# Attention output kept transposed and scaled on GpSimd through DRAM, with 14 loads a head, in a one-core attention and expert kernel

## The chip, the cores and the metric

The kernel runs on one core of a Trainium2 chip. The metric is the device time of one execution in microseconds. Three runs of the kernel before took 882.96, 883.56 and 879.89 us, median 882.96. One more execution was taken with the hardware profiler; it took 887.1 us.

The engines are named as in the profile: PE (TensorE, matmuls), PEld (its weight loads), DVE (VectorE), ACT (ScalarE), POOL (GpSimd) and SP (SyncE, which here only issues transfers).

## The reference

The input x is 4 images of 32 x 32 tokens with 192 channels. Two residual blocks follow one another: attention, then a mixture of experts.

```python
qkv = layernorm(x) @ qkv_w.T + qkv_b           # 12 heads of 16 channels
bias = rel_h[:, :, :, :, None] + rel_w[:, :, :, None, :]   # from q and two tables, 32 rows + 32 columns
attn = softmax((q * scale) @ k.T + bias, axis=-1)          # 1024 x 1024 for each of 48 (head, image)
x = x + (attn @ v) @ proj_w.T + proj_b
t = layernorm(x)                               # 4096 tokens
gate = t @ Wg.T + bg                           # 8 experts, the best one is taken
h = silu(t @ W1[e].T) * (t @ W2[e].T)          # F = 469
x = x + probability * (h @ W3[e].T)
```

What the change touches is the attention's output `attn @ v`: its division by the sums of the softmax, and the way in which it gets to the projection `@ proj_w.T`, where the 192 channels must lie on partitions.

## The kernel before

The program has stages that follow one another with a barrier between them: project (to about 116 us of the trace), attention (to 646 us), gate (to 709 us), route (to about 740 us) and experts (to the end).

Project normalizes x, makes q, k and v, splits q and k into a high and a low half-precision part each and stores them to DRAM (`qk_split`), as well as the products of q with the position tables (`rel_split`). v stays on the core.

Attention works on 48 (head, image) pairs, called heads here; n counts them, the image is n % 4. A head has four buffers' worth of slots, and the loads of head n + 3 are issued in step n. SP issues them: 8 loads of k and q parts (L526, L527, L530) after a wait for the scores of the head before, the rows of maxima (L621), and 8 loads of position products (L541, L542). On TensorE a step has four parts u = 0 to 3. In each, four score matmuls (L796) of the head, two raw-score tiles for maxima (L762) of a head ahead, and the weighted values (L808) of four tiles of probabilities. VectorE takes the maximum of each raw tile (L913), eight a head, from two PSUM buffers. GpSimd copies the eight maxima four times (L658), TensorE transposes them (L787, in u = 1), ScalarE copies that out (L878), and SP stores it as a further row of the score operand. ScalarE takes the exponentials (L896) from three PSUM banks. The weighted values come out as 4 quarters of 32 rows x 256 queries: 16 channels, one row of sums and unused rows in each quarter. Sums come from a seventeenth column of ones in v.

The output's way is: ScalarE copies it out of PSUM (copy_out, L884), TensorE turns it by 16 small matmuls against the identity (turn_out, L819, in u = 2 of the next head), VectorE takes the reciprocal of the sums (L923) and multiplies (L928) into `att_sb`, tokens on partitions.

GpSimd also does work for the experts in the attention steps, in program order after the copies of the head: the W3 weights of 8 experts are split into high and low parts, one expert every five heads (L720, L721, store L722), and the tail and top rows of W1 and W2 (L681, L682, L687, L688, loads L697, L701). It copies the head's values with their column of sums into a zeroed buffer (L666).

Gate has 8 steps of 512 tokens. TensorE first turns `att_sb` (8 transposes a step, L1073), ScalarE copies the result (L1138), then TensorE projects (L1084), VectorE adds the residual (L1192) and takes the statistics; normalization, parts and gate products follow some steps behind.

A list of instructions for each engine is fixed when the kernel is built; the engines wait for one another by semaphores.

## Time and profile before

| | us |
|---|---|
| three runs | 879.89, 882.96, 883.56 |
| profiled execution | 887.1 |
| its span | 884.8 |
| PE, DVE, ACT, POOL busy | 785.4, 724.5, 608.8, 284.8 |
| attention, from the trace | about 116 to 646 |
| gate, from the trace | 646 to 709 |

The span is the time between the first and the last record of the core, and 2.3 us of the execution lie around it. Busy times are of one engine each and overlap. A stage's limit is read from the stage: the steady period of a head, or of a step, and the wait that ends last in it. TensorE's granted clock was full (1.00) between 300 and 400 us, which is its higher level of 2.4 GHz.

### The profile page before, as it was taken

Reading aid. Unit: us, or ns where it says so; the run is one execution under the profiler, and the core shown is the slowest. Engines: PE = TensorE matmul, PEld = TensorE weight load, DVE = VectorE, ACT = ScalarE, POOL = GpSimd, SP = SyncE. Lnnn points to the kernel's source line nnn. Section 1 sums busy time; section 2 is a strip of 40 time slices with the busy share of each in tenths; the row PEclk is TensorE's granted clock in tenths of the full one; section 3 lists DMA queues with packets and bytes.
Section 4 is the critical chain, followed back from the end, with each engine's and each line's share of the span. In section 5 each row is a group of like instructions: output and inputs, shape, how many; then the busy total and the mean of one; then the engine's idle time right before and its main releaser. Section 6 shows DMA issues by size and latency. Waiting matters only on the chain. (4 is left out here: it accounts for less than half of the span.)

```text
span 884.8 us, 32156 instructions
## 1 busy us (share of the span) xinstructions
PE 785.4 (89%) x11946; PEld 487.2 (55%) x11946; DVE 724.5 (82%) x1022; ACT 608.8 (69%) x1139; POOL 284.8 (32%) x437
## 2 busy tenths in 40 slices
PE   3999938999999999999999999999988617999994
PEld 1768802444444444444444444444478617999994
DVE  6876767998999999999999999899347485888883
ACT  3675605888888888888888888888845603544442
POOL 5530000023343423303232233421015304666662
PEclk9999956999999999999999999999989657999998
DMA  6255973345555545444454545543044402222310
GB/s 175 72 144 176 365 225 101 101 126 135 137 145 139 134 128 135 125 120 129 135 137 132 140 135 145 150 125 84 4 179 133 166 0 75 81 82 83 97 57 8
DMA packets 69738, 109.71 MB, mean 124 GB/s; under 512 B 20139, under 2 KB 36681, under 8 KB 68146
## 3 DMA queue, kind: packets, MB, share of 16 engines
q1 hardware_dynamic: 59120, 75.49, 30.5%
q0 software_dynamic: 9248, 26.51, 10.6%
q10 hardware_dynamic: 1314, 6.95, 2.1%
q8 instruction: 36, 0.59, 0.3%
q14 instruction: 20, 0.16, 0.1%
HBM read 77.58 MB, written 33.19 MB: 125 GB/s over the span
## 5 line engine op out<-in xcount | busy, mean ns | idle before, releaser
L913 DVE TENSOR_REDUCE neg_max<-max_ps 128x1 f16<-128x1024 f32 x384 | 451.9, 1221 | 41.6 <-PE max_ps L762 33.9
L896 ACT ACTIVATE probs<-ring_ps 128x512 f32<-128x512 f32 x768 | 413.7, 596 | 68.7 <-PE ring_ps L796 60.0
L796 PE MATMUL ring_ps<-q_side,k_side 113*32 113x512 f16 x3072 | 241.1, 386 | 11.6 <-DMA q_side<-rel_split 8.3
L808 PE MATMUL out_ps<-probs,values 128*32 128x256 f32 x3072 | 200.4, 380 | 0.2 <-ACT probs L896 0.2
L762 PE MATMUL max_ps<-k_side,q_side 48*128 48x256 f16 x1536 | 137.5, 280 | 18.0 <-ACT ident L871 9.3
L808 PEld LDWEIGHTS out_ps<-probs,values 128*32 128x32 f32 x3072 | 92.7, 110 | 70.9 <-issue 1.0
L796 PEld LDWEIGHTS ring_ps<-q_side,k_side 113*32 113x32 f16 x3072 | 73.2, 94 | 96.8 <-ACT probs L896 38.7
L658 POOL COPY max_copies<-neg_max 128x32 f16<-128x32 f16 x48 | 10.1, 210 | 350.4 <-DVE neg_max L913 350.4
L762 PEld LDWEIGHTS max_ps<-k_side,q_side 48*128 48x128 f16 x1536 | 49.1, 95 | 121.9 <-issue 70.1
L1467 PE MATMUL hid_ps<-slot_t,w_top 128*118 128x128 f16 x312 | 69.0, 221 | 0.8 <-ACT slot_t L1513 0.8
L1468 PE MATMUL hid_ps<-slot_t,w_top 128*118 128x128 f16 x312 | 68.8, 221 | 0.0
L1471 PE MATMUL hid_ps<-slot_t,w_tail 128*118 128x128 f16 x312 | 68.8, 221 | 0.0
L1469 PE MATMUL hid_ps<-slot_t,w_top 128*118 128x128 f16 x312 | 68.8, 220 | 0.0
L1470 PE MATMUL hid_ps<-slot_t,w_tail 128*118 128x128 f16 x312 | 68.8, 220 | 0.0
L1446 POOL DMA_INDIRECT out<-y,slot_token x39 | 42.0, 1076 | 47.7 <-issue 25.7
L1431 POOL DMA_INDIRECT slot_rows<-token_rows,slot_token x39 | 44.2, 1133 | 39.4 <-issue 39.4
L1530 ACT ACTIVATE hidden_hi<-hidden 118x512 f16<-118x512 f32 x39 | 24.6, 631 | 40.1 <-DVE hidden L1570 40.1
L1570 DVE TENSOR_TENSOR hidden<-hid_ps,silu 118x512 f32<-118x512 f32 x39 | 27.0, 692 | 22.2 <-PE hid_ps L1471 17.0
L1523 ACT ACTIVATE silu<-hid_ps 118x512 f32<-118x512 f32 x39 | 23.3, 597 | 28.0 <-PE hid_ps L1471 28.0
L1467 PEld LDWEIGHTS hid_ps<-slot_t,w_top 128*118 128x118 f16 x312 | 41.9, 134 | 1.0 <-issue 1.0
L1468 PEld LDWEIGHTS hid_ps<-slot_t,w_top 128*118 128x118 f16 x312 | 42.0, 135 | 0.0
L1469 PEld LDWEIGHTS hid_ps<-slot_t,w_top 128*118 128x118 f16 x312 | 41.9, 134 | 0.0
(230 smaller groups left out, 1357.0 us busy)
## 6 DMA issues: line engine op xcount, KB each, us to landing
q_side<-rel_split SPq DMA_DIRECT2D x384, 64.0 KB, 2.3
q_side<-qk_split SPq DMA_DIRECT2D x192, 64.0 KB, 2.5
rel_split<-expert_weights ACTq DMA_DIRECT2D x6, 1024.0 KB, 4.9
rel_split<-expert_weights SPq DMA_DIRECT2D x6, 1024.0 KB, 6.1
q_side<-qk_split SPq DMA_DIRECT2D x48, 128.0 KB, 2.8
k_side<-qk_split SPq DMA_DIRECT2D x144, 32.0 KB, 1.8
token_rows<-tn_parts SPq DMA_DIRECT2D x8, 512.0 KB, 3.4
expert_weights<-in_w_t POOLq DMA_DIRECT2D x32, 117.2 KB, 3.0
```

Source lines behind the costliest of these rows:

```text
L762: last = nc.tensor.matmul(max_ps[t % 2][:, keys], q_side[j][at:at + HIGH, quarter, t * P:(t + 1) * P], k_side[j][at:at + HIGH, keys], star ...
L796: last = nc.tensor.matmul(ring_ps[turn_of(k) % BANKS][at:at + COLS, :], k_side[slot(s)][:, tile * P + at:tile * P + at + COLS], queries, s ...
L808: last = nc.tensor.matmul(out_ps[quarter * 2 * HD:(quarter + 1) * 2 * HD, :], values[j][:, tile, :], probs[:, u % 2 * GROUP + 2 * i + quar ...
L896: nc.scalar.activation(probs[:, u % 2 * GROUP + i, :], ring_ps[turn_of(k) % BANKS][:], ACT.Exp).then_inc(exp_done, 1)
L913: nc.vector.tensor_reduce(neg_max[:, j % 2, t:t + 1], max_ps[t % 2][:], AX, ALU.max, negate=True).then_inc(tile_max, 1)
L1431: pool.indirect_dma_start(rows[:, j, :], None, g.token_rows, bass.IndirectOffsetOnAxis(ap=g.slot_token[:, n:n + 1], axis=0), bounds_check= ...
L1446: pool.indirect_dma_start(g.out_rows, bass.IndirectOffsetOnAxis(ap=g.slot_token[:, n:n + 1], axis=0), y[:, j, :], None, bounds_check=last_ ...
L1467: nc.tensor.matmul(out, w_top[:, j, h, 0, some], hi_top, start=True, stop=False, skip_group_check=True)
L1468: nc.tensor.matmul(out, w_top[:, j, h, 0, some], lo_top, start=False, stop=False, skip_group_check=True)
L1469: nc.tensor.matmul(out, w_top[:, j, h, 1, some], hi_top, start=False, stop=False, skip_group_check=True)
L1470: nc.tensor.matmul(out, w_tail[:, j, h, some], hi_tail, start=False, stop=False, skip_group_check=True)
L1471: last = nc.tensor.matmul(out, w_tail[:, j, h, some], lo_tail, start=False, stop=True, skip_group_check=True)
```

## The change

The turned output is no longer made. The weighted output stays transposed (channels on partitions), and the values buffers are filled with ones, so that the sums come out in 16 rows of each quarter. For each head:

- ScalarE copies the output to `out_t`, which now has two buffers.
- SP stores one row of sums of each quarter to DRAM and loads them as 128 x 8; VectorE takes the reciprocal; SP stores it and loads it again, spread over 32 rows of each quarter. These four transfers are distributed over the steps of this and the next heads.
- GpSimd multiplies `out_t` by the spread inverse (`scale_output`).
- SP places the result in a DRAM buffer `att_dram`, channels by tokens. In steps 28 to 31 and in step 47 eight transfers bring it back, as `att_t` with channels on partitions. The last head of each image is placed directly by four transfers within the core's memory, three of the four in the gate stage.

The loads of a head go from 16 to 14: low and high k parts come in one transfer, and two position loads in one. SP's loop of four heads is written out as 48. The gate stage projects from `att_t` and has no transposes and copies.

```diff
+    sp.dma_start(k[K_LO:K_LO + 2 * HD, :], g.qk_split[1, :, rows, :]).then_inc(inc, 16)
+    sp.dma_start(k[0:HD, :], g.qk_split[1, 1, rows, :]).then_inc(inc, 16)
...
+    if i:
+        both = g.rel_split[1, :, :, head, slot, :].rearrange("q (a r) n -> r q a n", a=2)
+        sp.dma_start(q[HD + HS:HD + 2 * HS, :, :], both).then_inc(inc, 16)
...
+def store_sums(sp, g, n):
+    sp.wait_ge(g.out_copied, n + 1)
+    sp.dma_start(g.sums_dram[n % 2], g.out_t[HD::2 * HD, n % 2, :]).then_inc(g.sums_stored[n % 2], 16)
...
+def spread_inverse(sp, g, n):
+    sp.wait_ge(g.inverse_stored[n % 2], 16 * (n // 2 + 1))
+    every_row = g.inverse_dram[n % 2].rearrange("q (o n) -> q o n", o=1).broadcast_to([4, 2 * HD, N // 4])
+    sp.dma_start(g.spread[:, n % 2, :], every_row).then_inc(g.inverse_spread[n % 2], 16)
...
+def scale_output(nc, pool, g, n):
+    pool.wait_ge(g.inverse_spread[n % 2], 16 * (n // 2 + 1))
...
+    nc.gpsimd.tensor_tensor(g.scaled[:, n % 2, :], g.out_t[:, n % 2, :], g.spread[:, n % 2, :], ALU.mult).then_inc(g.output_scaled, 1)
...
+def place_output(sp, g, n):
+    sp.wait_ge(g.output_scaled, n + 1)
...
+        by_quarter = g.att_dram[head, :, image * N:(image + 1) * N].rearrange("c (q n) -> q c n", q=4)
+        sp.dma_start(by_quarter, g.scaled[:, n % 2, :]).then_inc(g.placed[n % B], 16)
...
+                if s.before(3):
+                    place_output(sp, g, s.n - 3)
+                if s.before(2):
+                    store_inverse(sp, g, s.n - 2)
+                if s.before(1):
+                    store_sums(sp, g, s.n - 1)
+                if s.after(3):
+                    load_positions(sp, g, head(s, 3), slot(s, 3), 0)
                 if s.after(1):
                     store_max(s.n + 1, slot(s, 1))
+                if s.before(2):
+                    spread_inverse(sp, g, s.n - 2)
+                if s.before(1):
+                    load_sums(sp, g, s.n - 1)
                 if s.after(3):
-                    load_positions(sp, g, head(s, 3), slot(s, 3))
-
-            steps(sp, BH, SLOTS, step)
+                    load_positions(sp, g, head(s, 3), slot(s, 3), 1)
...
+            for n in range(BH):
+                step(Step(n, n // SLOTS, n % SLOTS, BH, True))
...
-                nc.gpsimd.tensor_copy(values[slot(s)][:, :, 0:VW], g.v_sb[:, head(s) + slot(s) * HEADS]).then_inc(values_ready, 1)
+                nc.gpsimd.tensor_copy(values[slot(s)][:, :, 0:HD], g.v_sb[:, head(s) + slot(s) * HEADS]).then_inc(values_ready, 1)
                 if s.after(1):
                     repeat_max(s.n + 1, slot(s, 1), s.before(1))
+                if s.before(2):
+                    scale_output(nc, pool, g, s.n - 2)
...
-                    if u == 2 and s.before(1):
-                        bank_free(s, TURNED_AT)
-                        turn_out(s.n - 1)
...
-                    if u == 2 and s.before(1):
-                        normalize(s.n - 1, head(s, -1), slot(s, -1), s.before(2))
+                    if u == 0 and s.before(2):
+                        invert_sums(nc, dve, g, slot(s, -2), head(s, -2), s.before(4))
...
             def project_out(s):
-                pe.wait_ge(at_ready, 2 * s + 2)
+                if s % 2 == 0:
+                    pe.wait_ge(g.outputs_loaded[s // 2], 32)
+                    pe.wait_ge(g.last_placed[s // 2], 64)
```

In the order of instructions, SP's list in one step of attention stood like this before (k_side and q_side are the score operands of a head, rel_split the position products; the rest of the step is six more position loads):

```order
L526 ISA [waits scores_ready]
L526 DMA k_side<-qk_split 16x1024
L526 ISA
L526 DMA k_side<-qk_split 16x1024 x2
L527 REGISTER_ALU
L527 DMA q_side<-qk_split 16x4x1024
L530 DMA q_side<-qk_split 16x2x1024
L530 ISA
L530 DMA q_side<-qk_split 16x2x1024 x3
L620 REGISTER_ALU
L621 DMA q_side<-max_rows 1x32x128 [waits max_copied]
```

The same step stands like this now:

```order
L522 DMA k_side<-qk_split 32x1x1024 [waits scores_ready]
L523 DMA k_side<-qk_split 16x1024
L524 DMA q_side<-qk_split 16x4x1024
L527 DMA q_side<-qk_split 16x2x1024 x4
L605 DMA att_dram<-scaled 4x32x256 [waits output_scaled]
L573 DMA inverse_dram<-inverse 128x8 [waits inverted]
L549 DMA sums_dram<-out_t 4x256 [waits out_copied]
L537 DMA q_side<-rel_split 16x2x1024 x2
L539 DMA q_side<-rel_split 16x2x1024
L697 DMA q_side<-max_rows 1x32x128 [waits max_copied]
L581 DMA spread<-inverse_dram 128x1x256 [waits inverse_stored1]
L556 DMA sums<-sums_dram 128x8 [waits sums_stored0]
```

Five transfers for the output stand among the loads now, each with a wait of its own, and the rows of maxima stand between the position loads instead of ahead of all of them.

On GpSimd, in a step with a W3 split and a tail split (the names are those of the weights; values is the buffer of the next head), this stood before:

```order
L658 COPY max_copies<-neg_max 128x32 [waits tile_max,max_t_ready]
L720 CAST w_parts<-w_whole 128x768 [waits w3_stored,w3_loaded]
L721 TENSOR_TENSOR w_parts<-w_whole,w_parts 128x768 [waits weights_split]
L722 DMA w_split<-w_parts 128x1536 [waits weights_split]
L681 CAST expert_weights<-expert_weights 128x469 [waits tail_loaded0]
L682 TENSOR_TENSOR expert_weights<-expert_weights 64x469 [waits weights_split]
L697 DMA expert_weights<-in_w_t 64x469 [waits weights_split]
L697 DMA expert_weights<-in_w_t 64x469
L666 COPY values<-v_sb 128x8x17 [waits group_done]
```

and this stands now:

```order
L754 COPY max_copies<-neg_max 128x32 [waits tile_max,max_t_ready]
L595 TENSOR_TENSOR scaled<-out_t,spread 128x256 [waits placed2,inverse_spread0]
L819 CAST att_t<-att_t 128x768 [waits w3_stored,w3_loaded]
L820 TENSOR_TENSOR att_t<-att_t 128x768 [waits weights_split]
L821 DMA w_split<-att_t 128x1536 [waits weights_split]
L779 CAST expert_weights<-expert_weights 128x469 [waits tail_loaded0]
L780 TENSOR_TENSOR expert_weights<-expert_weights 64x469 [waits weights_split]
L795 DMA expert_weights<-in_w_t 64x469 [waits weights_split]
L795 DMA expert_weights<-in_w_t 64x469
L762 COPY values<-v_sb 128x8x16 [waits group_done]
```

The product of the output stands between the copy of the maxima and the splits, and waits for the spread inverse.

## Rows read from the trace of the kernel before

**Rows 1.** Windows of attention: busy us and count by engine, clock, DMA share, GB/s.
```profile
300.00:400.00 100.00, 98.95 (x1704) 45.90 (x1706) 93.67 (x96) 87.91 (x175) 29.39 (x53) 1.00 0.47 128
```

**Rows 2.** Timeline of PE, the transposed maxima: start, us, engine, line, operation.
```profile
283.01 0.22 PE L787 MATMUL ring_ps<-ident,max_copies 128*32 128x128 f16 x1
293.35 0.22 PE L787 MATMUL ring_ps<-ident,max_copies 128*32 128x128 f16 x1
```

**Rows 3.** Timeline of DVE in one head, with idle time before and its releaser.
```profile
286.33 0.20 DVE L923 RECIPROCAL recip<-ring_ps 128x8 f32<-128x8 f32 x1
...
286.88 4.78 DVE L913 TENSOR_REDUCE neg_max<-max_ps 128x1 f16<-128x1024 f32 x4
291.89 4.86 DVE L913 TENSOR_REDUCE neg_max<-max_ps 128x1 f16<-128x1024 f32 x4 [0.23 <-PE max_ps L762]
```

**Rows 4.** Timeline of SP, DMA issues in several stretches.
```profile
25.50 0.59 SPq L225 DMA_DIRECT2D qk_split<-expert_weights  x1
...
133.62 0.42 SPq L541 DMA_DIRECT2D q_side<-rel_split  x1
134.08 0.42 SPq L542 DMA_DIRECT2D q_side<-rel_split  x1
...
268.16 1.85 SPq L526 DMA_DIRECT2D k_side<-qk_split  x3
...
382.27 1.30 SPq L526 DMA_DIRECT2D k_side<-qk_split  x3
```

**Rows 5.** Waits of the whole span: waiter, releaser, total us, count, longest.
```profile
SPq L621 <- ACT max_rows L878: 87.6, 48, 9.6
```

**Rows 6.** Timeline of POOL in a step with W3 and tail splits.
```profile
250.06 0.83 POOL L720 CAST w_parts<-w_whole 128x768 f16<-128x768 f32 x1
...
256.63 0.30 POOL L666 COPY values<-v_sb 128x136 f32<-128x136 f32 x1
```

**Rows 7.** Windows of the gate stage, columns as in rows 1.
```profile
654.00:662.00 8.00, 8.00 (x54) 7.92 (x53) 4.76 (x19) 2.36 (x5) 0.00 (x0) 0.96 0.54 183
...
680.00:690.00 10.00, 8.62 (x75) 8.27 (x74) 7.14 (x26) 4.46 (x9) 4.25 (x9) 0.83 0.45 152
```

**Rows 8.** Timelines of PE and ACT in the head from 391.65.
```profile
391.26 0.39 PE L796 MATMUL ring_ps<-q_side,k_side 113*32 113x512 f16 x4
...
396.50 1.04 PE L808 MATMUL out_ps<-probs,values 128*32 128x256 f32 x16
...
397.73 0.27 ACT L878 ACTIVATE max_rows<-ring_ps 32x128 f16<-32x128 f32 x1
```

**Rows 9.** DMA, window 23 to 29: queue's packets, MB, share; KB, us to landing.
```profile
q1 hardware_dynamic: 448, 0.39, 21.4%
...
qk_split<-expert_weights SPq DMA_DIRECT2D x2, 128.0 KB, 2.0
```

**Rows 10.** Groups of lines in attention on POOL: busy us, mean ns, idle before.
```profile
L688 POOL TENSOR_TENSOR expert_weights<-expert_weights 128x469 f16<-128x469 f32 x16 | 17.3, 1080 | 1.4
...
L721 POOL TENSOR_TENSOR w_parts<-w_whole,w_parts 128x768 f16<-128x768 f32 x8 | 13.2, 1644 | 0.7
```

**Rows 11.** The page's DMA issues: count, KB each, us from issue to landing.
```profile
q_side<-qk_split SPq DMA_DIRECT2D x48, 128.0 KB, 2.8
```

**Rows 12.** DMA, window 266 to 268: the queue of instruction packets.
```profile
q8 instruction: 1, 0.02, 3.8%
```

**Rows 13.** Groups of lines in the gate stage, the transposes.
```profile
L1073 PE MATMUL at_ps<-ident_sb,att_sb 128*96 128x128 f32 x64 | 10.1, 310 | 2.5 <-ACT at_bottom L1138 1.6 <-PEq L566 0.9
```

**Rows 14.** Timeline of the gate stage.
```profile
646.32 1.05 PE L1073 MATMUL at_ps<-ident_sb,att_sb 128*96 128x128 f32 x8 [0.91 <-PEq L566]
...
650.43 0.55 PEld L1084 LDWEIGHTS proj_ps<-proj_w_top,at_top 96*128 96x128 f32 x2
...
682.82 1.01 DVE L1192 TENSOR_TENSOR x_sb<-proj_ps,x_sb 128x384 f32<-128x384 f32 x2
```

**Rows 15.** DMA, window 300 to 400: SP's queue.
```profile
q1 hardware_dynamic: 7620, 9.73, 37.0%
```

224 lines of the change are left out of this document (121 added, 103 removed).

## The prediction

> **What bounds the kernel now.** I read the windows of the two stages that the change touches, first, then one head of attention engine by engine, then the queues. All sums are made on the profiled execution, 887.1 us (span 884.8 and 2.3 around it), which lies 4.1 us above the median of 882.96 that is to be predicted; a difference found on the first is carried to the second. The three runs differ by 3.7 us among themselves, so 0.5% (4.4 us) is about what can be told from no change.
>
> In attention TensorE shows 98.95 us busy of 100 [rows 1], but it is not what sets the pace: its work is pipelined, and it waits on buffers that VectorE empties. One head takes 293.35 - 283.01 = 10.34 us, from one transposition of the maxima to the next [rows 2]. VectorE does eight maxima in it, four in 4.78 us and four in 4.86 (1.195 us each as they overlap), then a reciprocal and a product out of PSUM; between the last maximum and the first of the next head lie 0.55 us, and only 0.23 us is a wait on TensorE [rows 3]. So VectorE holds the head: 4.78 + 0.23 + 4.86 + 0.5 = 10.3.
>
> Three engines run close behind. SP issues 17 transfers for each head: where they stand written out, one starts at 133.62 and the next at 134.08, so one in 0.46 us [rows 4], some 8 us of the 10.3, and most of the rest is the wait for the rows of maxima, 87.6 us in 48 heads, 1.8 each [rows 5]. GpSimd is idle for 70% of the stretch [rows 1], but in lumps: in a heavy head it goes from a W3 split that starts at 250.06 through a tail split to the values copy that ends at 256.93, with no gap but its own chain [rows 6]. The gate stage is another matter: between 654 and 662 TensorE is busy 8.00 us of 8.00 [rows 7].
>
> **The change, part by part.** Attention, engine by engine. I call S the moment when the scores of the previous head are all done (391.65 in the head shown, from 391.26 + 0.39 [rows 8]).
>
> VectorE loses the reciprocal and the product between PSUM and att_sb, 0.55 us a head, and gains a reciprocal of the same 128x8, from SBUF, which I price at the 0.20 us of the one removed [rows 3]. TensorE loses 16 small matmuls, which stood ahead of the maxima that VectorE waits 0.23 us for. VectorE's own floor is then 9.6 + 0.2 + a short wait, about 9.95 us, -0.39 a head. ScalarE's 16 exponentials and two copies stay: 87.91 us of 100 [rows 1], 9.1 a head, so it does not become the limit.
>
> SP goes from 17 issues a head to 20: 14 loads, the maxima, and five for the new way of the output (sums out, sums in, inverse out, inverse spread, output placed). Sixteen of them at 0.46 are 7.4 us, and four that touch 128 rows I price at the 0.59 us of a 128-row store of before [rows 4]: 2.4. Together 9.8 us, with next to no time left for its waits. So a head cannot be shorter than about 9.8 to 10.1 us, and can be longer if a wait is met: place and inverse wait on other engines that are early, but the spread waits for a store that was issued some 2.7 us before and takes 2.0 us to land (the price of a 128-row store [rows 9]). I take 10.1 us, -0.24 a head, where VectorE alone would give 9.95; the ends are 9.95 and 10.5 (four waits of 0.1 more). For the 36 heads with a steady period: -8.5 us.
>
> The new product on GpSimd, 128x256. The trace has products of 768 elements in 1.644 us and of 469 in 1.080 [rows 10], so 1.9 ns an element, and 256 take 0.68 us. The engine has room, but the place counts: it stands behind the copy of the maxima and ahead of the weight splits and of the next values copy. SP reaches the spread after seven product loads (3.3 us), place, inverse, sums, three position loads, and the maxima, which are ready at S + 6.35 (397.73 + 0.27 [rows 8]). The spread is issued at about S + 7.2, lands 2.8 us later (the price of a 128 KB load [rows 11]), the product ends at S + 10.7, and with SP's own lag of some 0.3 us at S + 11.0. Before, GpSimd began its splits at S + 4.4. TensorE takes the next head's values at its S + 4.85 (396.50 [rows 8]), so the splits and the values copy now have 10.1 + 4.85 - 11.0 = 4.0 us. The heavy heads need 6.8 (256.93 - 250.12 [rows 6]). There are five with W3 and a tail split together, of 6.3 to 6.8 us: 32.7 - 20 = 12.7 us of loss. Nine others of 4.2 to 5.5 us lose 0.6 each on average, 5.6 together. TensorE has nothing to do in that wait and VectorE sits behind its two buffers, so this loss is on the path: +18 us. Its bounds: with the spread landing in 2.0 us and no lag the splits have 4.9 us and the loss is 9; with 3.6 us to land it is about 30.
>
> SP's code. The loop of four heads becomes 48 written out, so its instructions are fetched anew. Before, an instruction packet in the window 266 to 268 goes with three k loads that take 1.85 us where they otherwise take 1.30 [rows 4, 12]. I count +1.5 us for the first eight heads, where GpSimd's and VectorE's own fetches already make SP late, and +2 for later fetches (four to six times 0.5), bounds 0 and 5. Eight loads of the placed output add 8 x 0.5 us of issue in five heads: +2, bounds 0 and 4. Two position loads fewer ahead of the first head: -1. The last three heads have no loads and gain VectorE's 0.35 each: -1.
>
> The gate. TensorE's 64 transposes go: 10.1 us busy and 2.5 waiting [rows 13], and ScalarE's 16 copies with them. At the stage's start the projection began at 650.43, after transposes from 646.32 on [rows 14]: with one step's own load and copy left out, 3.6 us earlier now, if the outputs are there. In the steps that follow, TensorE is full until 662 and still 86% busy from 680 to 690 [rows 7], so of the other six steps' transposes (7.6 us) I count 5.4. The sum is -9 us, bounds -5 and -12. The three last heads are scaled and placed beside the first gate steps: the last placement, issued in the third step, lands some 19 us into the stage by my count, and image 3 is projected from the seventh step on, whose first residual stood at 682.82 [rows 14], 36 us in and 27 with the gain. So it is hidden; were that cover gone it would cost up to 4. The end of attention loses the last turn and VectorE's 0.55 us behind it [rows 3]: -1. The project stage loses a GpSimd memset that nothing waited for: 0.
>
> Sum: -8.5 + 18 + 1.5 + 2 + 2 - 1 - 1 - 9 - 1 = +3 us. On the profiled execution that is 890.1, on the median 886.
>
> **Rivals.** (A) The new chain is absorbed, and the gain stays: the spread lands in 2.0 us, the splits lose 9, SP keeps up and a head takes 9.95. Sum: -13.9 + 9 + 1 - 9 - 1 - 2 = -16, 867 us. For it: 128 KB stores landed in 2.0 us [rows 9]; SP has 1.8 us of wait a head that it can give up [rows 5]. Against: 20 issues leave it nothing, and the splits' length is measured.
>
> (B) The transfers become the bound: the new ones lie unevenly on the 16 DMA engines. In 300 to 400 SP's queue filled 37.0% of the engines' time [rows 15], 3.8 us of each engine in a head if it lies evenly. The spread and the placed output move 128 KB in rows of 1 KB, and the merged k load 32 rows of 2 KB. If four engines had to carry the first two and two engines the third, the busiest would take 32 + 32 rows at 0.046 us each (6.0 us x 16 x 21.4% / 448 [rows 9]) and 14 more at 0.078 (100 x 16 x 37.0% / 7620 [rows 15]): 4 us more, 7.9 us of every 10.1 beside GpSimd's own transfers, and what is spread or loaded lands 0.8 us later or more. Then heads take 10.3, the splits have 3.2 us and lose 30: -1.3 + 30 + 1.5 + 2 + 2 - 1 - 1 - 9 - 1 = +22, less what a longer head gives back to GpSimd, say +20: 903 us. It decides from the point where a spread lands over 3.3 us after its issue. Against it: nothing in this trace shows an uneven queue, since the transfers of before all have slowest dimensions of 16, 32, 64 or 128 rows.
> The Trainium skill, page "DMA: Bandwidth & Descriptors", section "Why a DMA increments its semaphore by 16 and not by 1", says that a transfer uses the largest number of engines, up to 16, that divides the slowest dimension of both sides, and that transfers from SP take the lowest-numbered ones. By that rule the spread and the placement (four quarters on one side) would use 4 engines and the merged k load (two parts) 2, which is this rival; no run here shows it yet.
>
> (C) SP itself is the bound beyond what I count, at 0.5 us an issue and with a wait in each head: 10.5 a head, +6 instead of -8.5, while GpSimd has 0.4 us more in each heavy head and loses 14: +13.5, 896.
>
> **How the numbers follow.** Forecast, 886 us: 0.40, with a range of its own from 878 to 895 (the splits' loss 9 to 25). A, 867: 0.31. B, 903: 0.18. C, 896: 0.11. Within 0.5% is 878.5 to 887.4: over half of the forecast's case (0.21), a little of A and C (0.04): 0.25. Faster: A without its tail and a little of the forecast: 0.32. Slower: the rest, 0.43. The range that leaves out two in ten: from 865, which takes in most of A, to 906, beyond B's value.
>
> **What would show it.** Heads of 10.1 us where GpSimd has no split, and 12 to 13 us in the five heavy ones, with TensorE's matmuls of the weighted values waiting for the values copy there: the forecast. SP without idle time between heads. Heads of 9.95 and no wait for values: A. Packets of 1 KB rows on a few engines only, spread landing after 3.3 us or more, and waits of TensorE on loaded heads: B. The first residual 3 to 4 us after the gate's start instead of 7, and the stage some 9 us shorter: the gate's term. The forecast is wrong if the values copy is never late, or if all heads, heavy or not, are longer than before.

## The result, and the profile after

| | before | after |
|---|---|---|
| median, us | 883.09 (4 runs, 879.89 to 883.56) | 989.19 (4 runs, 987.1 to 989.91) |
| ratio, 95% interval | | 1.121 (1.1175 to 1.1246) |
| span of the profiled execution | 884.8 | 987.4 |
| first to last transposition of the maxima (47 heads) | 500.4 | 599.7 |
| from there to the end of the span | 255.9 | 261.6 |

The kernel became 12.1% slower. 886 us had been forecast, with 906 as the upper end of the range. The table's last rows come from the transposed maxima, once a head: before they ran from 128.47 to 628.90. After, the query for that tile gives operation, count, shortest, median and longest duration in ns, and first and last start in us:

```profile
L891 PE MATMUL ring_ps<-ident,max_copies x48: 218/219/314, 126.1 to 725.8; 128*32 128x128 f16 x48
```

So 99.3 us of the 102.6 were lost between heads: a mean head takes 12.76 us and took 10.65. The stretch from 300 to 400 that [rows 1] shows of before, and a bad head just behind it (busy us and count of PE, PEld, DVE, ACT, POOL, then clock, DMA share, GB/s):

```profile
300.00:400.00 100.00, 84.61 (x1288) 35.92 (x1288) 77.06 (x74) 74.46 (x146) 36.05 (x62) 0.95 0.52 136
401.00:412.00 11.00, 10.98 (x137) 4.57 (x141) 6.17 (x6) 6.41 (x13) 2.74 (x5) 0.73 0.32 91
```

No engine is busier, but for GpSimd with 6.7 us more, mostly of products. TensorE issued 1288 matmuls where it had issued 1704; some 155 of the difference are the 16 small ones a head that the change itself removes, the rest is lost pace. In the second row it is busy for 10.98 us of 11.00 at a granted clock of 0.73 in the mean, so part of the time at the lower of its two levels (1.2 instead of 2.4 GHz); between 300 and 400 the mean is 0.95, where it was 1.00 [rows 1]. Sixteen matmuls of the same kind, right behind a wait of 2.12 us and eight us later:

```profile
401.02 1.93 PE L912 MATMUL out_ps<-probs,values 128*32 128x256 f32 x16 [2.12 <-POOL values L762]
408.64 1.04 PE L912 MATMUL out_ps<-probs,values 128*32 128x256 f32 x16
```

So a stall is paid for again in the matmuls behind it. Over the whole run the scores and the weighted values kept TensorE busy for 471.7 us (L900 and L912) instead of 441.5 (L796 and L808 of before); what part of that lay on the path no run tells, but in e15 and e16 below, where the stalls are gone, the clock is 1.00 again.

The heads are not equally long. PE's timeline (start, us) shows three transpositions early on, and two with the loads of the placed output between them:

```profile
141.03 0.22 PE L891 MATMUL ring_ps<-ident,max_copies 128*32 128x128 f16 x1
151.19 0.22 PE L891 MATMUL ring_ps<-ident,max_copies 128*32 128x128 f16 x1
161.38 0.22 PE L891 MATMUL ring_ps<-ident,max_copies 128*32 128x128 f16 x1
...
513.74 0.22 PE L891 MATMUL ring_ps<-ident,max_copies 128*32 128x128 f16 x1
534.90 0.31 PE L891 MATMUL ring_ps<-ident,max_copies 128*32 128x128 f16 x1
```

The first two heads shown take 10.16 and 10.19 us, but they lie ahead of the first spread (issued at 164.2), so the new chain does not run in them yet. Of the 44 heads in which it runs, only the last (9.85) is under 10.3. Compared with the same heads of before, the seven with a W3 split lost 23 us together (they take 12.4 to 16.7), the 23 with a tail or top split 35 (median 11.8), the ten without any split 17 (median 11.4), and the four at the loads of the placed output 27 (68.6 instead of 41.8). So more than half of the loss lies in heads for which the forecast had none or little. The waits of the whole span (total us, count, longest) name what is late:

```profile
POOL scaled L595 <- DMA spread<-inverse_dram: 391.4, 48, 14.1
DVE neg_max L1003 <- PE max_ps L868: 151.0, 126, 6.0
...
SPq L581 <- DMA inverse_dram<-inverse: 53.0, 33, 6.9
SPq L697 <- ACT max_rows L967: 49.5, 28, 5.2
PE ring_ps L900 <- DMA q_side<-rel_split: 39.8, 31, 2.9
...
PE out_ps L912 <- POOL values L762: 31.3, 20, 3.9
```

GpSimd waits for the spread in every head. SP waits 53.0 us for the stored inverse, a wait that before did not have, and TensorE 39.8 for loaded positions, where it had waited 8.3, by the page of before:

```profile
L796 PE MATMUL ring_ps<-q_side,k_side 113*32 113x512 f16 x3072 | 241.1, 386 | 11.6 <-DMA q_side<-rel_split 8.3
```

How the waits close into a loop is read from one head with a W3 and a tail split, on SP (issues) and on GpSimd:

```profile
389.78 0.58 SPq L697 DMA_DIRECT2D q_side<-max_rows  x1
390.75 0.57 SPq L581 DMA_DIRECT2D spread<-inverse_dram  x1
403.45 0.58 SPq L697 DMA_DIRECT2D q_side<-max_rows  x1
404.07 0.57 SPq L581 DMA_DIRECT2D spread<-inverse_dram  x1
```

```profile
394.77 0.72 POOL L595 TENSOR_TENSOR scaled<-out_t,spread 128x256 f32<-128x256 f32 x1 [6.44 <-DMA spread<-inverse_dram]
395.44 0.82 POOL L819 CAST att_t<-att_t 128x768 f16<-128x768 f32 x1
...
400.68 0.29 POOL L762 COPY values<-v_sb 128x128 f32<-128x128 f32 x1
400.91 0.22 POOL L754 COPY max_copies<-neg_max 128x32 f16<-128x32 f16 x1
```

From one store of maxima to the next: 0.97 us to the issue of the spread, 4.02 until the product starts, 6.14 of product, splits and the values copy until the next head's maxima are copied, and 2.54 through TensorE's transposition and ScalarE's copy until SP stores them: 13.67 us. The next spread stands behind that store in SP's list. Every late microsecond thus comes back in the next head. Without the splits (395.44 to 400.68) the same loop would take 8.4 us, an estimate from these rows; it is shorter than a head then, so in the ten heads without splits other waits must hold, those of SP and of TensorE on loads.

The end of attention and the gate did not give what was forecast either (+5.7 instead of -10):

```profile
740.57 0.17 POOL L852 MEMSET expert_weights<- 128x48 f16 x1
...
748.16 0.98 PE L1164 MATMUL proj_ps<-proj_w_top,att_t 96*128 96x192 f32 x2 [7.36 <-PEq L645]
...
767.09 1.19 POOL L595 TENSOR_TENSOR scaled<-out_t,spread 128x256 f32<-128x256 f32 x1 [4.27 <-DMA spread<-inverse_dram]
```

GpSimd's last work of the stage ends at 740.74 and ScalarE's last copy at 741.24, and yet the projection starts only at 748.16, 7.4 us behind GpSimd; before, GpSimd had ended 17 us ahead of VectorE, and TensorE started 0.3 us behind VectorE (646.00, and 646.32 in [rows 14]). From the last transposition of the maxima to the start of the gate stage it is 22.4 us instead of 17.4, and from there to the sum that makes the gates 62.1 instead of 61.8, where 9 us less had been forecast. In the gate the products of the last heads wait for their spreads ahead of the normalization on the same engine.

### The profile page after: what moved, and what is told of

It reads as the page before. It is cut to its first block and busy times, and to the rows that moved or that the text cites. A ratio compares the mean times of both kernels' runs of the same rounds, so it can differ in the third digit from the quotient of the medians.

```text
span 987.4 us, 29463 instructions
## 1 busy us (share of the span) xinstructions
PE 806.7 (82%) x11114; PEld 472.0 (48%) x11114; DVE 713.6 (72%) x973; ACT 604.3 (61%) x1123; POOL 315.2 (32%) x485
## 5 line engine op out<-in xcount | busy, mean ns | idle before, releaser
L986 ACT ACTIVATE probs<-ring_ps 128x512 f32<-128x512 f32 x768 | 415.1, 595 | 104.3 <-PE ring_ps L900 99.3
L900 PE MATMUL ring_ps<-q_side,k_side 113*32 113x512 f16 x3072 | 255.5, 403 | 52.9 <-DMA q_side<-rel_split 39.8
L912 PE MATMUL out_ps<-probs,values 128*32 128x256 f32 x3072 | 216.2, 404 | 31.6 <-POOL values L762 31.3
L595 POOL TENSOR_TENSOR scaled<-out_t,spread 128x256 f32<-128x256 f32 x48 | 35.3, 736 | 391.4 <-DMA spread<-inverse_dram 391.4
L868 PE MATMUL max_ps<-k_side,q_side 48*128 48x256 f16 x1536 | 139.8, 291 | 17.6 <-DMA q_side<-rel_split 9.4
L912 PEld LDWEIGHTS out_ps<-probs,values 128*32 128x32 f32 x3072 | 95.2, 116 | 123.0 <-POOL values L762 44.5
L900 PEld LDWEIGHTS ring_ps<-q_side,k_side 113*32 113x32 f16 x3072 | 70.5, 97 | 163.0 <-issue 78.3
L868 PEld LDWEIGHTS max_ps<-k_side,q_side 48*128 48x128 f16 x1536 | 54.0, 98 | 118.8 <-issue 72.2
L967 ACT ACTIVATE max_rows<-ring_ps 32x128 f16<-32x128 f32 x48 | 12.8, 266 | 64.1 <-PE ring_ps L891 62.7
L1638 DVE TENSOR_TENSOR hidden<-hid_ps,silu 118x512 f32<-118x512 f32 x39 | 27.0, 692 | 22.3 <-PE hid_ps L1539 17.4
L1535 PEld LDWEIGHTS hid_ps<-slot_t,w_top 128*118 128x118 f16 x312 | 42.3, 136 | 1.0 <-issue 1.0
L1536 PEld LDWEIGHTS hid_ps<-slot_t,w_top 128*118 128x118 f16 x312 | 42.4, 136 | 0.0
L1539 PEld LDWEIGHTS hid_ps<-slot_t,w_tail 128*118 128x118 f16 x312 | 42.3, 136 | 0.0
```

What stands on the lines that cost most here:

```text
L868: last = nc.tensor.matmul(max_ps[t % 2][:, keys], q_side[j][at:at + HIGH, quarter, t * P:(t + 1) * P], k_side[j][at:at + HIGH, keys], star ...
L900: last = nc.tensor.matmul(ring_ps[turn_of(k) % BANKS][at:at + COLS, :], k_side[slot(s)][:, tile * P + at:tile * P + at + COLS], queries, s ...
L912: last = nc.tensor.matmul(out_ps[quarter * 2 * HD:(quarter + 1) * 2 * HD, :], values[j][:, tile, :], probs[:, u % 2 * GROUP + 2 * i + quar ...
L986: nc.scalar.activation(probs[:, u % 2 * GROUP + i, :], ring_ps[turn_of(k) % BANKS][:], ACT.Exp).then_inc(exp_done, 1)
L1535: nc.tensor.matmul(out, w_top[:, j, h, 0, some], hi_top, start=True, stop=False, skip_group_check=True)
L1536: nc.tensor.matmul(out, w_top[:, j, h, 0, some], lo_top, start=False, stop=False, skip_group_check=True)
```

## The experiments

The theories, numbered as in the expectations: (1) order: the product stands ahead of the splits and waits for a landing, a loop through GpSimd; (2) few engines: the spread, the placed output and the merged k load lie on few of the 16 DMA engines and delay what is queued with them (rival B); (3) SP: 19 to 20 issues and waits of its own in one ordered list. The ratio is always to the kernel before in runs on the same chip.

**e1: the product behind the splits.**

```diff
                 if s.after(1):
                     repeat_max(s.n + 1, slot(s, 1), s.before(1))
-                if s.before(2):
-                    scale_output(nc, pool, g, s.n - 2)
...
                     load_top(g, top, s.n)
+                if n >= 2:
+                    scale_output(nc, pool, g, n - 2)
```

> The product on GpSimd moves from ahead of the weight splits to behind them (and ahead of the next values copy), nothing else. Theory 1 (order): in the changed kernel the spread's landing and the product stand in a loop, SP's spread, product, splits, values and maxima copy, TensorE, ScalarE, SP's store of the maxima, spread again, so each head lasts as long as that loop (11.1 us with a tail split, 13.7 with W3 too). Behind the splits the landing is hidden: heads fall to the 10.2 to 10.5 us of SP's 20 issues, GpSimd's wait for the spread (391 us) falls below 200, and the time to 900 to 920 us; the four steps with loads of the placed output stay long. Theory 2 (few DMA engines): the transfers themselves are late, so the wait only moves; heads stay above 11.5 and the time above 945 us.

960.48 us, ratio 1.0876 (1.081 to 1.0941); a mean head takes 12.15. So the place is worth 29 of the 106 us, and 77 remain: not the 900 to 920 us of theory 1 alone. GpSimd's wait for the spread fell from 391 to 305 us only. SP's wait for the inverse stays:

```profile
SPq L581 <- DMA inverse_dram<-inverse: 52.4, 38, 4.5
...
PE ring_ps L900 <- DMA q_side<-rel_split: 62.7, 39, 4.2
```

**e2: the same transfers on more engines, e3: e1 and e2 together.** The k load is split again, the spread goes in four parts of 32 rows, the placed output lies in DRAM as 128 rows, and is loaded per head in 16 rows: 24 issues a head.

```diff
-    sp.dma_start(g.spread[:, n % 2, :], every_row).then_inc(g.inverse_spread[n % 2], 16)
+    for q in range(4):
+        sp.dma_start(g.spread[2 * HD * q:2 * HD * (q + 1), n % 2, :], every_row[q]).then_inc(g.inverse_spread[n % 2], 16)
...
-        sp.dma_start(by_quarter, g.scaled[:, n % 2, :]).then_inc(g.placed[n % B], 16)
+        sp.dma_start(g.att_dram[head, image], g.scaled[:, n % 2, :]).then_inc(g.placed[n % B], 16)
```

> The product stays ahead of the splits; every transfer that has a slowest dimension of 2, 4, 5 or 6 is reshaped so that it has 16 or more: the k load in two parts (15 loads), the spread in four parts, the placed output in rows of quarter and channel, and its loads head by head. SP has 24 issues a head. Theory 2 (few DMA engines): the spread lands in 2.8 us instead of 4.3 and the steps that load the placed output lose their stalls of 3 to 10 us each, and the attention stage ends 1.5 us after its last matmul instead of 7: 920 to 945 us. Theory 1 (order): the loop keeps its length but for the landing, and SP's 4 further issues (1.9 us) eat that: 955 to 985 us outside the four long steps' share, so at least 950.

> Both edits. If order and engines are separate losses, heads last as long as SP's 24 issues, 11.3 to 11.6 us, without heavy heads, and the time is 915 to 935 us. If order alone is the cause, it is slower than the kernel with the order alone by SP's 1.9 us a head, some 20 to 80 us; if engines alone, as fast as the one with the engines alone.

976.0, ratio 1.1051 (1.097 to 1.1133), and 967.71, 1.0957 (1.0891 to 1.1024). Both are slower than theory 2 and the sum of theories had it (920 to 945, and 915 to 935). The spread now lands 3.45 us after the first of its issues (4.1 in after, medians from issue to the product's start), but four more issues eat that: the median head of e3 takes 11.75, and 24 issues at 0.48 are 11.5. With e3 above e1, theory 2 looked refuted; by e14 to e16 below, the longer list had hidden it.

**e7: only the placed output in 128 rows and its loads by head, at 20 issues a head.**

```diff
-    sp.dma_start(g.att_t[0:HD * len(heads), c, tokens], g.att_dram[heads.start:heads.stop, 0:HD, tokens]).then_inc(g.outputs_loaded[image], 16)
+        sp.dma_start(dst, g.att_dram[head, image].rearrange("(q r) n -> r q n", q=4)[0:HD]).then_inc(g.outputs_loaded[image], 16)
```

> The changed kernel with only the placed output in rows of quarter and channel and loaded head by head in 16 rows. Theory 2: the four steps' stalls, 20 us together against their neighbours, fall to the 2.3 us of five more issues each, and the wait of 7 us at the end of attention goes; with placements on 16 engines the spread lands up to 1 us sooner: 950 to 965 us. Theory 1: the four steps stay long, since the loop through the spread is what is late there, and the time stays within 980 to 992.

959.62, ratio 1.0913 (1.0875 to 1.0951): 30 us back, as theory 2 had it. The spread still lands after 4.1 us. The four heads with output loads take 57.7 instead of 68.6, and SP's wait for the inverse falls from 53.0 to 25.6 us; 19 us of the gain lie in the other heads. That the old loads used few engines shows in after, in a window at the end of attention in which only such loads run (columns as above):

```profile
741.00:747.00 6.00, 0.00 (x0) 0.00 (x0) 0.00 (x0) 0.24 (x1) 0.00 (x0) 0.82 0.32 131
```

Four loads of 320 KB, with five heads as the slowest dimension on the DRAM side, are in flight together, and the share stays at 0.30 to 0.34 in each us from 741 to 750. Five of sixteen engines would be 0.31. By the Trainium skill, page "DMA: Bandwidth & Descriptors", section "Why a DMA increments its semaphore by 16 and not by 1", a transfer runs on the largest number of engines, up to 16, that divides the slowest dimension of both sides, which is five here; the trace agrees.

**e5: the chain stretched by one head** (four buffers of output, product and spread one head later, the spread at the end of SP's step), **e6: e5 with e7's edit, e8: e6 with the placement issued by GpSimd.**

```diff
+                if s.before(3):
+                    place_output(sp, g, s.n - 3)
...
+                if s.before(2):
+                    spread_inverse(sp, g, s.n - 2)
...
-                if s.before(2):
+                if s.before(3):
+                    scale_output(nc, pool, g, s.n - 3)
```

```diff
-                if s.before(3):
+                if s.n == BH - 1:
...
+                    if s.n - 3 < BH - B:
+                        place_output(pool, g, s.n - 3)
```

> The changed kernel with the output's chain stretched by one head, its transfers and sizes as they are: the spread is issued at the end of SP's step (behind all loads, so its wait stands in front of none of them), the product follows one head later at the place it had (out_t has four buffers, the product is written over the spread), and the placement stands behind the maxima. Theory 1 (order): neither the loop through GpSimd nor SP's wait for the inverse (53 us in the changed kernel, in 33 heads) is left, heads come down to SP's 20 issues, 10.2 to 10.5 us, except the four heads with loads of the placed output; time 895 to 915 us. Theory 2 (few DMA engines set the pace whatever the order): loads land late as before, heads stay above 11 us, time above 935 us.

> The stretched chain, and the placed output kept in rows of quarter and channel, so that its store has 128 rows on both sides and its loads come head by head in 16 rows (44 instead of 8); k load and spread stay on few engines. Theory 2 for the loads of the placed output: the four steps lose their stalls (20 us together) and the attention stage ends 1.5 us after its last instruction instead of 7: 865 to 890 us. If those steps were long for the order's sake, no further gain against the stretched chain alone.

> As the stretched chain with the placed output in rows, and in addition GpSimd issues the placement itself behind its product, so that SP has 19 issues a head. If SP's issues are what is left, heads come down by another 0.4 to 0.5 us, 18 to 22 us less than without this edit; if VectorE already holds the head at 10.0 us, no gain; if GpSimd's extra 0.9 us a head brings back late values in the heads with W3 and a tail split, these get longer by up to 1 us each.

945.58, ratio 1.0753 (1.0701 to 1.0806); 930.09, 1.0567 (1.0519 to 1.0615); 941.71, 1.0712 (1.0659 to 1.0766). Slack for the product gives 44 us, but no run comes near the forecasts of theory 1 (895 to 915) or of e6 (865 to 890), and e8, with an issue less on SP, is slower than e6 and not 20 us faster: SP's wait only changes its line. In e5 and in e8, where SP has an issue less (the second diff), it stands at the load of the sums:

```profile
SPq L556 <- DMA sums_dram<-out_t: 44.7, 35, 4.4
```

```profile
SPq L556 <- DMA sums_dram<-out_t: 60.7, 40, 4.7
```

**e9: e8 with all of SP's waits for landings at the end of its step, the output placed by quarters again and loaded in few large transfers, and in the gate stage the expert loads earlier and one more product; e10: after with the expert loads earlier in the gate stage.**

```diff
-                if s.before(1):
-                    load_sums(sp, g, s.n - 1)
...
+                if s.before(1):
+                    load_sums(sp, g, s.n - 1)
```

```diff
+            load_experts(sp, g, experts_loaded)
...
-                    load_experts(sp, g, experts_loaded)
```

> The stretched chain, with SP's list cut to 19 issues a head and every wait on a landing at its end: GpSimd issues the placement, the spread and then the load of the sums stand behind all loads. The placed output lies in rows of channels with one stride, so its 8 loads have 96 or 80 rows as slowest dimension. In the gate stage the loads of the expert weights come ahead of the last placements, and head 45's product moves from the end of attention to the gate's start. Theory 3 (SP's list is full and in order, 10.17 us of issue a head in the changed kernel, so that each of its waits lengthens the head): heads come down to VectorE's 9.9 to 10.1 us, except where GpSimd is late; attention is 20 to 25 us shorter than in the stretched kernel with rows, the barrier behind attention comes within 2 us, and the gate is 5 to 9 us shorter than before: 860 to 885 us. If few DMA engines (spread and k load are still on 4 and 2) make loads late whatever SP does, heads stay at 10.7 to 11.3 and the time above 905 us.

> The changed kernel with one move: the four loads of the expert weights go from behind the last placement in the gate stage to ahead of head 46's placement, as early as the chain allows. If these 3 MB are what makes the normalized rows late in the middle of the gate, the gate gets 4 to 7 us shorter and the time 982 to 985 us; if the last placements then come late, the gain is lost: 987 to 992 us.

938.95, ratio 1.0659 (1.0603 to 1.0715): no better than e8 within the intervals, and each run slower than each of e6. The wait has gone to the next engine with an ordered list, and SP waits 81.8 us for the inverse that comes of it:

```profile
DVE inverse L566 <- DMA sums<-sums_dram: 43.8, 35, 7.4
```

e10: 992.08, ratio 1.1248 (1.1181 to 1.1315), no gain. The way from the last transposition to the gates' sum is 83.3 us instead of 84.5, while GpSimd waits 9.10 us for the last spread instead of 4.27, so the last placement comes later. Whether the expert loads held the gate stays open.

**e4: before with the merged k load alone; e11: before with three tiny loads more in each head (20 issues).**

```diff
-    for at, src in ((0, k_hi), (K_LO, k_lo), (LOWER, k_hi)):
-        sp.dma_start(k[at:at + HD, :], src).then_inc(inc, 16)
+    sp.dma_start(k[0:HD, :], k_hi).then_inc(inc, 16)
+    sp.dma_start(k[K_LO:K_LO + 2 * HD, :], g.qk_split[1, :, bass.ds(slot * D + head * HD, HD), :]).then_inc(inc, 16)
```

```diff
+    for j in range(3):
+        sp.dma_start(g.spare[slot][:, 8 * j:8 * j + 8], g.rel_split[0, 0, 0:HS, head, slot, 0:8]).then_inc(inc, 16)
```

> The kernel before with one part of the change alone: low and high k parts of a head loaded by one transfer of 32 rows (15 loads a head instead of 16). Theory 2 in its strict form (two DMA engines carry it, and these two are late): heads get longer by 0.2 to 0.5 us, 890 to 905 us. Theory 1: one issue less on SP, which has 1.8 us of wait a head: 880 to 884 us, no change.

> The kernel before with three tiny loads more for each head (16 rows of 16 bytes into a spare buffer, issued behind the position loads; 20 issues a head on SP instead of 17, the count of the changed kernel), nothing else. If the count of issues alone costs what the changed kernel lost, heads go to 11 us and more and the time above 915 us. By theory 3 the count takes only the 1.8 us that SP waits in a head, since none of the new issues waits: heads of 10.3 to 10.6 us, 880 to 897 us.

e4: 883.23, ratio 1.0008 (0.9974 to 1.0043): the merged load costs nothing in the kernel before. e11: 898.46, ratio 1.0185 (1.0142 to 1.0229): three issues more that wait for nothing cost 17 us, and SP's slack for the maxima falls from 87.6 us [rows 5] to

```profile
SPq L623 <- ACT max_rows L880: 35.3, 32, 9.8
```

But TensorE counts these loads among those of the head and waits for the last of them:

```profile
PE ring_ps L798 <- DMA spare<-rel_split: 18.1, 19, 2.2
```

So three small loads a head, issue and landing together, cost a sixth of what the change cost; this run does not tell the two apart.

**e12 to e16: the waits and the uneven transfers taken away one after the other.** The number of issues and their bytes stay as in after (e14's and later ones' output loads are per head). The outputs are not divided by the right sums, and in e16 other rows of k are used too. Each cut of the diff is against the run before it. e12: the product is of `out_t` with itself, so it does not wait for this head's spread but for that of the head before. e13: the loads of sums and spread read inputs, so SP waits for no landing of this head's chain. e14: e7's edit. e15: the spread reads 128 rows. e16: the k load reads 32 rows that follow one another.

```diff
-    nc.gpsimd.tensor_tensor(g.scaled[:, n % 2, :], g.out_t[:, n % 2, :], g.spread[:, n % 2, :], ALU.mult)
+    nc.gpsimd.tensor_tensor(g.scaled[:, n % 2, :], g.out_t[:, n % 2, :], g.out_t[:, n % 2, :], ALU.mult)
...
-    sp.wait_ge(g.inverse_stored[n % 2], 16 * (n // 2 + 1))
-    every_row = g.inverse_dram[n % 2].rearrange("q (o n) -> q o n", o=1).broadcast_to([4, 2 * HD, N // 4])
+    every_row = g.w3_rows[0, 0:4, 0:N // 4].rearrange("q (o n) -> q o n", o=1).broadcast_to([4, 2 * HD, N // 4])
...
-    every_row = g.w3_rows[0, 0:4, 0:N // 4].rearrange("q (o n) -> q o n", o=1).broadcast_to([4, 2 * HD, N // 4])
+    every_row = g.w3_rows[0, :, 0:N // 4]
...
-    sp.dma_start(k[K_LO:K_LO + 2 * HD, :], g.qk_split[1, :, rows, :]).then_inc(inc, 16)
+    both = g.qk_split[1].rearrange("i r n -> (i r) n")[bass.ds(slot * D + head * HD, 2 * HD), :]
+    sp.dma_start(k[K_LO:K_LO + 2 * HD, :], both).then_inc(inc, 16)
```

> The changed kernel, with the product on GpSimd taken of the output with itself, so that it need not wait for the spread just issued (it waits for the one of the head before, which has landed); all transfers are still issued. What it leaves out: the division by the sums. Theory 1: the loop through GpSimd is gone and only SP's own wait for the inverse and its full list remain, 940 to 965 us, near the kernel whose product stands behind the splits (960). If GpSimd's wait costs nothing, above 980.

> As the kernel without the product's wait, and in addition the spread and the load of the sums read inputs of the same shape instead of what was just stored, so that SP waits for no landing of the chain either. The same 20 issues a head, the same bytes, the same few engines; left out: the division by the sums. If the waits for landings in the engines' ordered lists are the larger loss, it comes down to 905 to 930 us (20 issues cost 16 us in the kernel before, the four heads with loads of the placed output some 15, the gate 5). If the transfers themselves are the limit (uneven engines, late loads), it stays above 940 us.

> As the kernel with the chain cut, and the placed output in rows of quarter and channel, loaded head by head in 16 rows. If the transfers of the placed output on few engines are what is left besides the count of issues, 890 to 905 us; if not, no more than the 5 us that the end of attention gains.

> The kernel with the chain cut and the placed output in rows, and one thing more: the spread reads 128 different rows of an input instead of 4 rows 32 times, so that it moves the same 128 KB by the same one issue, but with a slowest dimension of 128 on both sides. Left out: the division by the sums. If the spread's place on 4 engines still makes the head's loads late (TensorE waited 47 us for position loads), 905 to 915 us and a shorter wait; if not, 920 to 926 as before.

> As the kernel with the even spread, and the merged k load reads 32 rows in a row instead of two times 16, so that it has a slowest dimension of 32 on both sides; same bytes, same issue. Left out besides the division: the right k rows (low parts stand where high parts should). Now no transfer of the head is on fewer than 16 engines but the 4 KB of sums. If uneven engines are what was left, 895 to 905 us, what 20 issues cost in the kernel before; if bytes and packets as such are, no change against the kernel with the even spread.

| | us | ratio (95%) | step |
|---|---|---|---|
| after | 989.19 | 1.121 (1.1175 to 1.1246) | |
| e12, no wait of GpSimd | 945.2 (a second run 961.35) | none | -44 |
| e13, no waits of SP for the chain | 930.81 | 1.0533 (1.0449 to 1.0617) | -14 |
| e14, placed output on 16 engines | 923.45 | 1.045 (1.0367 to 1.0532) | -7 |
| e15, spread on 16 engines | 886.67 | 1.006 (1.0029 to 1.009) | -37 |
| e16, merged k load on 16 engines | 881.55 | 1.0 (0.9977 to 1.0023) | -5 |

e12's two runs lie 16 us apart and the steps go by the shorter, so only the sum of the first two is firm, 58 us. The numbers of engines in the table are by the rule above. The 7 us of e14 are within the intervals of e13 and e14. The step to e15 is far outside them: of 923 us in e14, 37 (34 by the ratios) go with the shape of the spread, though each issue moves the same bytes and hardly anything of the chain is waited for but the loaded sums (VectorE, 12.5 us) and the inverse behind them (SP, 16.0). The spread, which from issue to use took 4.1 us in after, lands in e15 in

```profile
spread<-in_w_rows SPq DMA_DIRECT2D x48, 128.0 KB, 2.6
```

What the spread did to others shows in e14, in the loaded rows of a head, issued on SP and used on PE:

```profile
296.25 0.42 SPq L542 DMA_DIRECT2D q_side<-rel_split  x1
```

```profile
303.82 1.04 PE L908 MATMUL ring_ps<-q_side,k_side 113*32 113x512 f16 x8 [3.69 <-DMA q_side<-rel_split]
```

7.5 us lie between issue and use, with TensorE idle for the last 3.69; in the kernel before, the 64 KB position loads landed after 2.3 us in the median. TensorE's total wait for such loads in e14, e15 and e16, one row of each:

```profile
PE ring_ps L908 <- DMA q_side<-rel_split: 47.1, 29, 4.0
```

```profile
PE ring_ps L908 <- DMA q_side<-rel_split: 20.9, 22, 2.2
```

```profile
PE ring_ps L909 <- DMA q_side<-rel_split: 15.3, 17, 1.9
```

And it is not the bytes: from 150 to 550 after moved 131 GB/s at a share of 0.51, e16 more of both with no loss, at full clock:

```profile
150.00:550.00 400.00, 340.96 (x5070) 143.45 (x5066) 299.80 (x283) 290.38 (x567) 114.11 (x200) 0.93 0.51 131
```

```profile
150.00:550.00 400.00, 380.47 (x6030) 163.68 (x6030) 355.87 (x337) 344.33 (x675) 137.84 (x247) 1.00 0.62 158
```

Two things stay open. e15 also replaces four source rows that are each read 32 times by 128 rows, and no run tells that wholly apart from the engines; against it speaks e2, which reads the same four rows 32 times each, but in four transfers with 32 rows as slowest dimension, and whose product starts 2 us after the last of them is issued (the four issues take 1.97 us together). And in another order of removal the steps would have other sizes, since the same lateness is shared.

**e17: a complete version in which hardly anything waits for a fresh landing.** One transfer within the core's memory of 112 rows puts the sums beside the outputs (they stand 16 rows apart, in every quarter), VectorE inverts 112x256 in place, GpSimd multiplies a head later, the placed output goes by rows, and k in three loads: 19 issues.

```diff
+    sp.dma_start(g.spread[0:P - HD, n % 2, :], g.out_t[HD:P, n % 2, :]).then_inc(g.inverse_spread[n % 2], 16)
...
+    sums = g.spread[0:P - HD, slot % 2, :]
+    nc.vector.reciprocal(sums, sums).then_inc(g.inverted, 1)
```

> A kernel that computes the reference and keeps the transposed output, drawn from the findings: no transfer of a head on fewer than 16 engines and no wait on a fresh landing in an ordered list. One transfer within the core's memory moves rows 16 to 127 of the output to rows 0 to 111 (112 rows on both sides), which puts each quarter's sums beside its outputs and replaces four transfers through DRAM; VectorE takes the reciprocal of 112x256 two parts later, GpSimd multiplies one head later, the placement has 112 rows and the outputs are loaded head by head in 16 rows, one a step. 15 loads a head, 19 issues. If uneven engines and waits were the whole loss, heads take 10.2 to 10.4 us (VectorE's reciprocal is longer by some 0.15 us than the one of 8 columns), the gate is 5 to 9 us shorter than before, and the time is 865 to 880 us. If the added 400 KB a head as such cost, heads are above 10.6 and the time above 890 us.

914.02 us, ratio 1.0342 (1.03 to 1.0385). All heads, those with W3 splits too, are now alike, but long: 11.35, from PE's timeline, and the reason stands in the groups by line (busy us, mean ns, idle time before and its releaser):

```profile
303.55 0.22 PE L876 MATMUL ring_ps<-ident,max_copies 128*32 128x128 f16 x1
314.90 0.22 PE L876 MATMUL ring_ps<-ident,max_copies 128*32 128x128 f16 x1
```

```profile
L560 DVE RECIPROCAL spread<-spread 112x256 f32<-112x256 f32 x48 | 83.7, 1743 | 9.6 <-DMA spread<-out_t 9.6
```

1.74 us on the engine that holds the head, where 0.15 more than the old reciprocal had been expected: with the maxima of [rows 3], 4.78 + 4.86 + 1.74 are 11.38. The chain's landings are no longer the matter: VectorE waits for them 9.6 us in 48 heads, and between 150 and 550 not at all. The gate, by contrast, did what was forecast: from the last transposition of the maxima to the sum that makes the gates it took 79.2 us before, 84.5 in after, and 69.8 here.

**e18: e17 with the inversion as a power of -1 on GpSimd.**

```diff
-    nc.vector.reciprocal(sums, sums).then_inc(g.inverted, 1)
+    nc.gpsimd.tensor_tensor(sums, sums, g.minus[0:P - HD, 0:1].broadcast_to([P - HD, N // 4]), ALU.pow).then_inc(g.inverted, 1)
```

> The kernel with the shifted sums, whose heads all took 11.35 us because VectorE's reciprocal of 112x256 takes 1.74 us; here GpSimd takes the reciprocal instead, as a power with the exponent -1, in front of the copy of the maxima, where it is idle for some 4 us of a head. If that power takes under 3 us, heads fall to 10.2 us, the gate keeps its 9 us, and the time is 858 to 872 us, below both kernels. If it takes 5 us or more, it is late for the copy of the maxima in each head and heads go above 11 us again: over 900 us.

2557.55 us, ratio 2.8983 (2.8914 to 2.9051): a miss, as one such operation takes 41 us.

```profile
L560 POOL TENSOR_TENSOR spread<-spread,minus 112x256 f32<-112x256 f32 x48 | 1975.2, 41150 | 2.6 <-DMA spread<-out_t 2.5
```

No complete version was faster than the kernel before.

## Why the prediction was wrong

- **The undisturbed head**, 10.1 us, was right where nothing waits: in e16, with all 20 issues, 23 of 47 heads take 10.25 us or less, most of them 10.18 or 10.19. In after, only the last head with the chain running was under 10.3, so the sign that the prediction named against itself, all heads longer whether heavy or not, came true but for the last. VectorE's floor of 9.95 was not reached in e16 either.
- **The landings** were the first step that failed. The spread was priced at 2.8 us from a 128 KB load in even rows [rows 11]; from issue to the product's start it took 4.1 in the median. The store of the inverse was priced at 2.0 us [rows 9], issued 2.7 ahead, so that SP would not wait for it; it landed after 4.4 in after and after 1.7 in e16:

```profile
inverse_dram<-inverse SPq DMA_DIRECT2D x48, 4.0 KB, 4.4
```

```profile
inverse_dram<-inverse SPq DMA_DIRECT2D x48, 4.0 KB, 1.7
```

- **Rival B** was named with its mechanism and its sign, a spread that lands after 3.3 us, and the sign came. It got 0.18 because no transfer of before was uneven; that absence was no evidence against it, since the change made such transfers for the first time. Its size was wrong by half: +20, against the 42 us that e15 and e16 took off. It was worked out from the mean load of the busiest engine (7.9 us of 10.1). What counts is how late a load becomes that is queued with it, and for whom: 7.5 us in e14.
- **The splits' loss, "+18"**, took lateness as something that a window of 4.0 us absorbs and that ends with the head. In the heavy heads it is a loop: the spread is issued behind the maxima, which wait for the GpSimd list, which waits for the spread. e1 and e12, which open the loop in different places, are 29 and about 44 us faster.
- **SP's added waits** were held to be nothing ("place and inverse wait on other engines that are early", and the inverse's store landed by the time of the spread). The engines are early, but the store has to land: 53.0 us of waits in an ordered list with all loads behind it, on an engine whose issues fill the head (nineteen in 9.6 us, from 379.65 on). e12 and e13 together took 58 us off.
- **The count of issues** was in the head's 10.1, and e16 bears that out; e11 shows that SP's slack was worth something all the same, 17 us for three small loads more in before. The forecast let SP give its slack away without a loss.
- **The loads of the placed output**, +2: their four heads grew by 26.7 us, part of it what all heads lost. On few engines, as the window from 741 to 747 shows; e7 took 10.9 of it off, and even in e16 the four take 50.3 instead of 41.8.
- **The gate and the end of attention**, -9 and -1: the size was right (e17: 69.8 us instead of 79.2, -9.4), but in after nothing of it came (+5.7 from the last head to the end). The end of attention lost 5.0 us, as GpSimd ended late and the next stage began 7.1 us behind it; the gate stage kept its 62 us, as the last products and their landings stood ahead of the normalization: without their waits it takes 56.0 us in e13 and 54.3 in e14. The prediction had named this cover and priced its loss at up to 4.
- **SP's written-out code**, +3.5, was not measured by itself, and no row shows the share of the other engines' fetches in it. e16 has it, and its attention takes 505.5 us (125.8 to 631.3) instead of 500.4: 5 us for it, the added issues, the output's loads and the splits together, less what shorter heads gave back.

## What to carry to other kernels

Before a transfer is added, work out over how many DMA engines it spreads, from the slowest dimension on both sides, and put its price on the loads that share its queue. A wait for a landing in an engine's ordered list holds all that is behind it, and moving it to another engine moves the loss (SP in after, e5 and e8, VectorE in e9); follow it round until it either ends or comes back to its own start. A price read from transfers of one shape holds for that shape and for a queue as empty as it was. A gain at a stage's border counts only if no other engine becomes the one that the border waits for.

## What the runs showed of the hardware that was not expected

- A reciprocal on VectorE takes 1.743 us for 112x256, and 0.20 for 128x8 [rows 3]: 6.2 ns for each column more between these two sizes, so sums gathered on 128 rows are much cheaper than spread ones.
- A power on GpSimd takes 41.15 us for 112x256; a product of 128x256 takes 0.72.
- Behind a late GpSimd the next stage begins 7.12 us after GpSimd's last instruction, though all others have ended:

```profile
747.86 2.34 POOL L1121 MEMSET slot_rows<- 128x2688 f32 x1 [7.12 <-POOLq L645]
```

It is 7.12 in after, e1, e2, e3, e5, e6, e7 and e10 alike (10.71 in e8, where GpSimd also issues the placements), and 0.3 us behind the last of the others where GpSimd ended about 9 us or more before the next stage, as in before, e9 and e13 to e17. What GpSimd does in that time no trace shows.
